# Attention weights of the later queries added on GpSimd ahead of the row sums, with a ring of twelve heads

## What is computed

```python
scores = jnp.einsum('bqhd,bkhd->bhqk', q, k) * scale
scores = jnp.where(causal[None, None], scores + bias[None], jnp.finfo(scores.dtype).min)
attn = jax.nn.softmax(scores, axis=-1)
out = jnp.einsum('bhqk,bkhd->bqhd', attn, v).reshape(B, S, H)
return out @ w_proj + b_proj
```

## Time and profile before

| | us |
|---|---|
| median of three runs | 1267.71 |
| lowest and highest | 1266.81, 1270.55 |
| the profiled execution, time | 1269.12 |
| its span | 1267.3 |
| PE busy | 1114.0 (88%) |
| DVE busy | 869.7 (69%) |
| ACT busy | 630.5 (50%) |
| POOL busy | 387.9 (31%) |

### The profile page before, as it was taken

One profiled execution on the slowest core, in us unless ns is written; L12 is line 12 of the kernel. 1 busy time (PEld: TensorE's weight loads), 2 busy tenths in 40 slices (PEclk: granted clock), 3 DMA queues, 4 the chain that ended last, 5 costly groups with the idle time before them and its releaser, 6 DMA issues. The chain is left out here.

```text
span 1267.3 us, 31645 instructions
## 1 busy us (share of the span) xinstructions
PE 1114.0 (88%) x12161; PEld 914.5 (72%) x12161; DVE 869.7 (69%) x2188; ACT 630.5 (50%) x1433; POOL 387.9 (31%) x561
## 2 busy tenths in 40 slices
PE   6569998779979995657799999999999999999987
PEld 5446776657778994546557888888888888888776
DVE  6466997778846678767476677667766776664574
ACT  4434555331433664547644554555455545553654
POOL 3331123076710155771055016202620261000120
PEclk9769999687989998777999999999999999999998
DMA  7737885222279886462343234223343332232001
GB/s 175 187 115 208 221 226 193 100 79 84 80 262 418 320 301 225 144 178 100 112 105 98 85 111 126 85 85 114 121 152 90 117 114 88 90 102 80 1 18 50
DMA packets 77986, 176.17 MB, mean 139 GB/s; under 512 B 12614, under 2 KB 26182, under 8 KB 75270
## 3 DMA queue, kind: packets, MB, share of 16 engines
q1 hardware_dynamic: 71564, 157.09, 38.8%
q0 software_dynamic: 6272, 17.05, 4.4%
HBM read 112.82 MB, written 61.08 MB: 137 GB/s over the span
## 5 line engine op out<-in xcount | busy, mean ns | idle before, releaser
L2373 ACT ACTIVATE decay<-masked,negcum 128x128 f32<-128x128 f32 x512 | 163.0, 391 | 102.1 <-DVE mixT L2437 102.1
L2281 PE MATMUL joint<-xh,w_high 128*128 128x512 f32 x512 | 209.3, 409 | 2.2 <-POOL wl L2217 2.2
L2281 PE MATMUL joint<-xl,w_high 128*128 128x512 f32 x512 | 200.2, 391 | 0.0
L2281 PE MATMUL joint<-xh,wl 128*128 128x512 f32 x512 | 199.8, 390 | 0.0
L2485 DVE COPY cT<-joint 128x512 f32<-128x512 f32 x128 | 88.3, 690 | 85.7 <-PE joint L2281 85.4
L2391 ACT ACTIVATE bT<-joint 128x512 f32<-128x512 f32 x128 | 76.7, 599 | 130.8 <-PE joint L2281 130.8
L2437 DVE TENSOR_TENSOR mixT<-pcb,decay 128x512 f32<-128x512 f32 x128 | 82.4, 685 | 55.8 <-PE pcb L2297 55.7
L2214 POOL TENSOR_TENSOR w_high<-w_in,none 128x512 fp32r<-128x512 f32 x32 | 35.0, 1094 | 261.4 <-DMA w_in<-in_w_bc 250.8
L2281 PEld LDWEIGHTS joint<-xh,w_high 128*128 128x128 f32 x512 | 96.1, 188 | 23.9 <-POOL wl L2217 2.6
L2281 PEld LDWEIGHTS joint<-xh,wl 128*128 128x128 f32 x512 | 96.1, 188 | 20.7
L2281 PEld LDWEIGHTS joint<-xl,w_high 128*128 128x128 f32 x512 | 96.3, 188 | 17.0
(11 more groups left out here) (367 smaller groups left out, 2711.7 us busy)
## 6 DMA issues: line engine op xcount, KB each, us to landing
cumrow<-ssm_cum SPq DMA_DIRECT2D x128, 256.0 KB, 3.3
slots_in<-blank SPq DMA_DIRECT2D x16, 1024.0 KB, 5.5
rows<-slots_in SPq DMA_DIRECT2D x32, 512.0 KB, 5.3
slots_out<-spare SPq DMA_DIRECT2D x32, 512.0 KB, 3.9
weights<-in_expert_quads SPq DMA_DIRECT2D x16, 768.0 KB, 9.1
w_in<-in_w_bc SPq DMA_DIRECT2D x32, 256.0 KB, 3.7
qk_parts<-parts SPq DMA_DIRECT2D x32, 192.0 KB, 2.3
stack<-qk_parts SPq DMA_DIRECT2D x32, 192.0 KB, 5.3
```

Source lines behind the costliest of these rows:

```text
L2281: last = nc.tensor.matmul(bank[:], w[:, j, col:col + P], a[:, k, c * CHUNK:(c + 1) * CHUNK], start=(m == 0), stop=(m == len(parts) - 1))
L2373: last = nc.scalar.activation(decay[:, n % 2, o], masked[:, n % 2, o], ACT.Exp, bias=negcum[:, c * TPC + i, head:head + 1])
```

## The change

GpSimd gets a step of its own for each head, fold: when the head's weights are there, it adds the two blocks of weights of the late queries (columns 128 to 255 and 256 to 383 of probT) into a new ring late. The product with ones then has no need to run over both: for key block 0 it takes only the early queries (128 columns in place of 256), and for key block 1 it takes late. The products with vpad stay as they are. The number of matmuls stays the same. values waits for the folds of its eight heads (folded) and no longer for the exponentials.

To make room, the ring of weights holds twelve heads in place of sixteen: 12 x (384 + 128) columns is what 16 x 384 were. The wait of weigh for values is rewritten for that: steps 0 to 3 of a unit need the values of two units before, steps 4 to 7 those of the unit before.

POOL's loop over units becomes a loop over steps, so that the folds stand between what it did already: split at step 1, ahead of that step's fold, and the work for the norms at step 4, ahead of that step's fold.

```diff
-HELD = 2 * HALF
+HELD = 3 * HALF // 2
...
+        late = sb("late", [P, HELD, P])
...
+                def fold(n):
+                    pool.wait_ge(exped, n + 1)
+                    nc.gpsimd.tensor_tensor(late[:, n % HELD, :], probT[:, n % HELD, P:S], probT[:, n % HELD, S:3 * P],
+                                            ALU.add).then_inc(folded, 1)
...
+                for i in range(-LEAD * HALF, STEPS + 2 * HALF):
+                    n = i + LEAD * HALF
+                    if n % HALF == AT_BLOCK and 0 < n // HALF <= UNITS:
+                        split(n // HALF - 1)
+                    if n % HALF == AT_ADD and 0 < n // HALF <= UNITS + 2:
+                        norm_work(n // HALF - 1)
+                    if 0 <= i < STEPS:
+                        fold(i)
...
-                    pe.wait_ge(exped, (u + 1) * HALF)
+                    pe.wait_ge(folded, (u + 1) * HALF)
...
+                                    held = (u * HALF + odd * QUADS + g) % HELD
                                     left_side = (vpad[:, 2 * seq + m, h * VW:(h + 1) * VW], ones[:, odd, :])[side]
+                                    if side == 0:
+                                        cols, moving = slice(lo, S), probT[:, held, col:col + S - lo]
+                                    elif m == 0:
+                                        cols, moving = slice(0, P), probT[:, held, 0:P]
+                                    else:
+                                        cols, moving = slice(P, S), late[:, held, :]
...
-                        act.wait_ge(pv_done, n // HALF - 1)
+                        act.wait_ge(pv_done, (n - HELD) // HALF + 1)
```

More of the change, by code:

```diff
@@ L502, in stage_attention @@
         projected, y_ready = chip.sem("projected"), chip.sem("y_ready")
-        blank_set = chip.sem("blank_set")
+        blank_set, folded = chip.sem("blank_set"), chip.sem("folded")
         norm_chain, norm_link = chip.sem("norm_chain"), chip.sem("norm_link")
@@ L579, in split, with norm_work @@
                                             ).then_inc(max_split, 1)
-                for u in range(UNITS + 2):
-                    if u < UNITS:
-                        split(u)
+                def fold(n):
+                    pool.wait_ge(exped, n + 1)
+                    nc.gpsimd.tensor_tensor(late[:, n % HELD, :], probT[:, n % HELD, P:S], probT[:, n % HELD, S:3 * P],
+                                            ALU.add).then_inc(folded, 1)
+                def norm_work(u):
                     g = chunk_at(u, Y_MEASURE + 1)
@@ L641, in values @@
                                     h = k * HALF + 2 * g + odd
+                                    held = (u * HALF + odd * QUADS + g) % HELD
                                     left_side = (vpad[:, 2 * seq + m, h * VW:(h + 1) * VW], ones[:, odd, :])[side]
+                                    if side == 0:
[4 more added lines that the diff above has]
+                                        cols, moving = slice(P, S), late[:, held, :]
                                     last = nc.tensor.matmul(
-                                        po[u % 2][g * VW:(g + 1) * VW, side, lo:S], left_side,
-                                        probT[:, (u * HALF + odd * QUADS + g) % HELD, col:col + S - lo],
+                                        po[u % 2][g * VW:(g + 1) * VW, side, cols], left_side, moving,
                                         start=(not odd and m == 0 and side == 0), stop=(odd == 1 and m == 1),
```

## The result

| | before | changed |
|---|---|---|
| median of 20 runs, us | 1266.34 | 1272.80 |
| lowest and highest, us | 1262.17, 1274.33 | 1267.09, 1276.95 |
| ratio | | 1.0044, interval 1.0028 to 1.0060 |

The changed kernel is slower by 0.44%, 5.6 us by the ratio (the two medians lie 6.5 us apart), and the interval (3.5 to 7.6 us) excludes a change of zero. The forecast was 1270.4, +2.7 us, "within 0.3%" with a chance of 0.51 and "slower" with 0.42. The range held the time, but of these two statements the one with the smaller chance came true.

A forecast was written before the change was run, and what follows sets the result against it. PE and VectorE are both nearly full: VectorE sets plain stretches, PE counts in projecting ones. Costs of 3.95 us against gains of 2.8 net +1.2; one clock drop of 1.5 makes +2.7, from 1267.7 to 1270.4, range 1264.5 to 1275.5.

The forecast's parts named there:

- Plain stretches are VectorE's, projecting ones PE's: Attention stage: PE's saving counts 0.44 us each in projecting units 3, 5, 7, 11, nothing in plain 4, 6, 8, 10.
- Unit 2: Unit after the queries' DMA wait, VectorE idling 2.31 us behind it, PE's clock partly low: 0.65 us saved, an estimate.
- The ordinary fold is hidden: Units without norm work: a fold takes 0.42 us, 0.48 start to start, and ends 0.1 to 0.2 before values.
- POOL as the bound: Rival, chance 0.15: folds take 0.62 us and GpSimd sets the ordinary unit; 1275, or 1276.5 with a clock drop.
- Norm work ahead of due folds: GpSimd's step 4: norm work delays folds and so values; +1.75 us in unit 9, +0.5 in 12, +1.65 in 13.
- The clock: PE idle about 2 us in units 9, 12, 13; each hole may cost 0 to 1.7; one drop taken at 1.5.
- three drops: Rival, chance 0.20: all three PE holes cost a clock drop, with folds at 0.42 us; +6 us, 1273.7.
- Units 14 and 15: Stage's tail: unit 14 saves 0.35 us after its last fold; unit 15 costs 0.05, a 0.5 fold less 0.44 saved.
- DVE is left alone by it as far as rows show: Cost of a fold on GpSimd: it was taken not to slow VectorE; no size was given.

The follow-up runs named there:

- e2: Changed kernel without any fold, values waiting for the exponentials, late queries' row sums lacking key block 0; ratio to the kernel before 0.9981.
- e5: Folds and narrow products in units 2, 3, 5, 7 and 11 alone, all other units as before the change; ratio to the kernel before 0.9987.
- e6: Folds and narrow products in units 4, 6, 8 and 10 alone, all other units as before the change; ratio to the kernel before 0.9993.
- e1: Changed kernel with GpSimd's norm work moved from step 4 back to step 1, right behind the split; ratio to the kernel before 1.0013.
- e11: Changed kernel plus 30 unread products of 128 columns on PE before the values of unit 13; ratio to the kernel before 1.0076.
- e3: Changed kernel with two VectorE subtractions of 128x768 moved from units 14 and 15 to behind the last values; ratio to the kernel before 1.0067.

## Why the prediction was right and wrong

- **Plain stretches are VectorE's, projecting ones PE's: right.** Plain ones did not shrink (7.36 against 7.37), units 3, 7 and 11 gave 0.42, 0.43 and 0.42 with 0.44 forecast, and e2, e5 and e6 show the same from three sides. Unit 5 gave 0.08; PE waited there for DMAs, 0.51 us the longest. Unit 2 gave 1.19 with 0.65 taken; it includes the 0.57 by which turn 4 came later.
- **The ordinary fold is hidden: right.** 0.46 us in place of 0.42, 0.41 from one to the next in a queue in place of 0.48. POOL as the bound, the slower rival, falls: the point at which it decides (0.52) was reached by none but the two slow folds below.
- **Norm work ahead of due folds: right.** Late by 1.49, 1.59 and 1.85 in units 9, 12 and 13, where the sum had 2.2, 1.95 and 2.1 (the queue runs off faster than taken). From the turns: unit 9 cost 1.12 net (forecast 1.75), unit 12 0.28 (0.5). e1 took off 3.75 us in the stage and 3.9 in the times; in the stage that is this term (3.0) and the clock behind unit 13 (1.6), less 0.9 by which turn 11 came later.
- **The clock: right mechanism, too few.** One drop at 1.5 was taken, as a choice between none and three. There were two: behind unit 13 (1.63 by e11, 1.62 by e1) and in unit 15, where the clock was 0.58 from 223 to 226 (1.68: 8.90 us to the last project in place of the 7.22 of e11). Units 9 and 12 had holes of 1.49 and 1.59 us and no drop, and e11 had none behind 1.78, so length alone does not tell.
- **Units 14 and 15: the step that failed.** The prediction took -0.35 and +0.05 for them. From turn 15 to the last project the stage goes from 1.07 us ahead to 4.87 behind: 1.48 and a clock drop of 1.63 are unit 13, which was forecast nearly so; the rest belongs to units 14 and 15. The sentence at fault is "DVE is left alone by it as far as rows show": the question was asked from the side of VectorE alone. From the side of GpSimd, two folds took 1.07 and 1.09 us because VectorE was reading two operands from SBUF. e3 puts 1.25 us on it. Unit 14 cost 0.3 (0.72 of wait less the saving), unit 15 0.8 (a wait of 1.78 against 0.58 for the exponential, less the saving) and the second drop 1.68 behind it: 2.8 in place of -0.3.
- **The sum.** Forecast +2.7. Units 14 and 15 were 1.4 dearer than taken, the second drop adds 1.7 and the first was 0.1 dearer; units 9, 12 and 13 were cheaper by 0.6, 0.2 and 0.2, unit 5 gave 0.4 less, and units 4 and 10, at 0, came out 0.5 shorter by what moves by itself. That makes 4.8, and the last project begins 4.87 later. The 4.20 at the next stage are what the higher clock on the last project leaves of it.
- **The time: in range, in part by luck.** 1272.8 is only 2.4 above the forecast of 1270.4, but the change is about twice the forecast one, +5.6 against +2.7. The starting point, 1267.7 from three runs, came out at 1266.3 from twenty. And the upper end of the range stood where it did for two rivals, POOL as the bound and three drops, neither of which came.
- **What the stage does not show.** The 5.6 of the times is 1.4 more than the profiled stage shows. The profiled execution is one of the shortest; over the twenty runs a lower mean of the granted clock tends to go with a longer time (0.935 to 0.938 in the four fastest of the changed kernel, 0.928 to 0.934 in the ten slowest). That holes in other units cost the clock in those runs would fit, but no profile shows it, and e11, whose profiled stage is only 1.4 us longer than before and whose ratio is 1.0076, speaks against it. Of the chain above, then, the term of the norm work is borne out by the times (e1); what the slow folds and the clock drops cost is read from profiles alone. This part stays open.

## What to carry to other kernels

An addition that is free on an idle engine is free only if its due time is looked up in that engine's queue: here 2.4 us of work that nobody had waited for became the path because four short additions that were already due stood behind it. Before moving work to GpSimd, list VectorE's instructions with two SBUF operands that run at the same time, and look at what any GpSimd instruction beside them takes. And do such work only where it pays: with five units of sixteen the kernel is at best slightly faster (0.9987, interval to 0.9999), with all sixteen slower (1.0044).

## What was not expected of the hardware

- A GpSimd addition of 128x128 f32 takes 457 ns alone and 1.07 to 1.10 us when it meets a VectorE subtraction of 128x768 with both operands in SBUF (0.95 us). VectorE's maxima, with one operand in PSUM, don't do this: once the two subtractions are moved (e3), none of 128 folds takes more than 487 ns.
- Additions of GpSimd that stand ready one behind the other overlap: five in 2.12 us, 0.41 from start to start, shorter than one takes.
- A hole of 1.85 us ahead of unit 13 was followed by the lower clock at a price of 1.63 us, and holes of 1.49 and 1.59 us ahead of units 9 and 12 by none. A hole of 1.78 us ahead of unit 15 was followed by it in the changed kernel and in e1, and not in e11.
